# The decay exponentials of quarter 1 in front of the silu of z of quarter 1, in ScalarE's order of a delta-rule attention and FFN kernel

## What is computed

```python
mixed = silu(conv4(x @ W_qkv.T));  z = x @ W_z.T
q, k = l2norm(q), l2norm(k)
decay = exp(where(tril, gc[i] - gc[j], 0)) * tril          # gc: running sum of the log decay, in a chunk
A  = -(k_beta @ k.T * decay) * strict;  Tm = inv(I - A)
u  = Tm @ v_beta;  kcd = Tm @ (k_beta * exp(gc))
for each chunk:
    attn  = (q_i @ k_i.T) * decay_i
    v_new = u_i - kcd_i @ S
    out_i = (q_i * exp(g_i)) @ S + attn @ v_new
    S     = S * exp(g_last) + (k_i * exp(g_last - g_i)).T @ v_new
out = rmsnorm(out) * norm_w * silu(z);  y = out @ W_out.T
x = x + layernorm(y);  x = x + layernorm(ffn(layernorm(x)))
```

## Time and profile before

| | |
|---|---|
| time, median of 3 runs | 4530.6 us (4528.2 to 4533.37) |
| the profiled execution | 4533.44 us, of it 4531.0 us span |
| TensorE | 4297.6 us busy (95% of the span) |
| TensorE weight loads | 3229.5 us (71%) |
| VectorE | 3523.2 us (78%) |
| ScalarE | 2981.9 us (66%) |
| GpSimd | 2987.7 us (66%) |
| DMA | 275.17 MB, mean 61 GB/s |
| granted TensorE clock, mean | 0.985 |

### The profile page before, as it was taken

How to read it: one execution, slowest core, us unless ns; L and a number is a source line. 1 busy time by engine, 2 the same in 40 slices (tenths; PEclk the granted TensorE clock), 3 DMA queues, 4 the chain that set the end, 5 groups by cost and what they waited for, 6 DMA issues and landing times. The chain is left out here.

```text
span 4531.0 us, 93023 instructions
## 1 busy us (share of the span) xinstructions
PE 4297.6 (95%) x30676; PEld 3229.5 (71%) x30676; DVE 3523.2 (78%) x8064; ACT 2981.9 (66%) x6124; POOL 2987.7 (66%) x8711
## 2 busy tenths in 40 slices
PE   5899999999999999999999999999999999998898
PEld 2577777777777777777777777777777777776444
DVE  6688888888888888878888788878888888885554
ACT  3577777777777767766777767766777767774111
POOL 1677777777777777777777777777777777774000
PEclk7899999999999999999999999999999999999899
DMA  4222222222222222222222222222232222210200
GB/s 133 56 65 60 67 67 46 67 59 68 67 57 65 60 67 59 55 71 64 67 67 55 64 63 59 62 68 60 67 75 47 69 58 69 64 36 20 71 14 19
DMA packets 592240, 275.17 MB, mean 61 GB/s; under 512 B 464400, under 2 KB 548880, under 8 KB 582544
## 3 DMA queue, kind: packets, MB, share of 16 engines
q1 hardware_dynamic: 591040, 266.62, 23.9%
q0 software_dynamic: 720, 2.62, 0.3%
HBM read 221.84 MB, written 47.28 MB: 59 GB/s over the span
## 5 line engine op out<-in xcount | busy, mean ns | idle before, releaser
L714 DVE SCALAR_TENSOR_TENSOR CV<-pp,CW,CV 128x1023 f32<-128x1023 f32 (+2 forms) x768 | 980.3, 1276 | 33.1 <-ACT CV L1076 21.8
L339 PE MATMUL pp<-A,W 128*128 128x512 f32 x2048 | 970.4, 602 | 30.1 <-DVE CV L714 18.8
L1373 POOL TENSOR_TENSOR UL<-UL,TM 128x126 f32<-128x126 f32 (+22 forms) x1984 | 743.4, 375 | 155.4
L1370 POOL TENSOR_TENSOR TM<-UL,XL 128x126 f32<-128x126 f32 (+22 forms) x1984 | 708.5, 357 | 147.2 <-issue 12.6
L339 PEld LDWEIGHTS pp<-A,W 128*128 128x128 f32 x2048 | 377.7, 193 | 338.8 <-issue 307.2
L1172 ACT ACTIVATE QE<-qa,TAB 128x128 f32<-128x128 f32 x1024 | 318.2, 362 | 407.9 <-PE qa L468 407.8
L834 DVE SCALAR_TENSOR_TENSOR St<-St,TAB,kv 128x128 f32<-128x128 f32 x1024 | 309.0, 343 | 325.0 <-PE kv L487 317.2
L1183 ACT ACTIVATE VS<-qa,EB 128x128 f32<-128x128 f32 x1024 | 319.1, 364 | 300.5 <-PE qa L478 294.7
L510 PE MATMUL emit<-Wz,A 128*128 128x256 f32 x2048 | 492.0, 383 | 4.3 <-DVE A L885 4.1
L531 PE MATMUL emit<-Wo,NTr 128*128 128x256 f32 x2048 | 493.7, 384 | 1.3 <-ACT NTr L1216 1.3
L1076 ACT ACTIVATE CV<-pp,CW 128x1024 f32<-128x1024 f32 x256 | 285.0, 1113 | 231.2 <-PE pp L339 231.2
(11 more groups left out here) (220 smaller groups left out, 9242.3 us busy)
## 6 DMA issues: line engine op xcount, KB each, us to landing
GB<-gcd SPq DMA_DIRECT2D x64, 1024.0 KB, 4.9
W<-wqkv SPq DMA_DIRECT2D x256, 128.0 KB, 3.7
XL<-xb SPq DMA_DIRECT2D x128, 256.0 KB, 3.9
UL<-c_u SPq DMA_DIRECT2D x64, 256.0 KB, 2.9
xb<-X SPq DMA_DIRECT2D x512, 32.0 KB, 1.7
Wz<-wz SPq DMA_DIRECT2D x64, 256.0 KB, 2.8
ub<-UL SPq DMA_DIRECT2D x128, 128.0 KB, 2.9
N<-ub SPq DMA_DIRECT2D x256, 64.0 KB, 2.3
```

Source lines behind the costliest of these rows:

```text
L339: ins = t.matmul(bk.pp[:, 512 * h:512 * h + 512], m.W[:, c, k, :], m.xnT[:, w // KH % 2, c, 512 * h:512 * h + 512], start=c == 0, stop=c == 1)
L714: v.scalar_tensor_tensor(m.CV[:, t, d:S], bk.pp[:, 0:S - d], m.CW[:, w % KH, t, 3 - d:4 - d], m.CV[:, t, d:S], ALU.mult, ALU.add).then_inc ...
L1370: gp.tensor_tensor(m.TM[:, 0:a, 0:b], m.UL[:, 0:a, k:k + 1].to_broadcast([128, a, b]), m.XL[:, k, k + 1:32].unsqueeze(1).to_broadcast([128 ...
L1373: gp.tensor_tensor(m.UL[:, 0:a, k + 1:32], m.UL[:, 0:a, k + 1:32], m.TM[:, 0:a, 0:b], ALU.subtract).then_inc(s["sub"], 1)
```

## The change

In the body of ScalarE's loop the call `dec(u + 1, 1)` moves one place forward, ahead of `sz(u - 1, 1)`. (ScalarE's loop counts one iteration later than TensorE's, so these are the decay factors of one unit and the silu of the unit two before it.)

```diff
@@ -1306,8 +1306,8 @@
             dec(u + 1, 0)
             vs(u - 1, 5)
             vne(u - 1, 5)
+            dec(u + 1, 1)
             sz(u - 1, 1)
-            dec(u + 1, 1)
             qe(u - 1, 6)
             sq(u - 1, 2)
             nt(u - 1, 1)
```

## The result

| | before | after |
|---|---|---|
| median | 4531.8 us (4528.2 to 4533.4, 4 runs) | 4566.8 us (4565.1 to 4568.5, 4 runs) |
| ratio | | 1.008, 95% interval 1.0068 to 1.0092 |
| span of the profiled execution | 4531.0 us | 4562.7 us |

What follows compares the result with a forecast made beforehand. TensorE, busy 2929.0 of 3000 us, was taken as the bound. Terms +0.93, -0.22, -0.10 and +0.07 made +0.68 us a unit, times 62 about 43 us: 4574 us against the median 4530.6, range 4555 to 4602.

Steps and rivals of the forecast that it cites:

- silu of quarter 1 later: ScalarE, quarter 1: with the four exponentials first, the silu starts at 2098.43 instead of 2097.23, 1.20 us later.
- shift of TensorE behind the transpose: TensorE at L520: the transpose of `CO` waits for the later norm, +0.93 us a unit.
- given back at `op`: TensorE at `op`: it no longer waits for ScalarE's `NTr`, -0.22 us a unit.
- given back at `z` of quarter 2: TensorE at `z` of quarter 2: its wait for VectorE's `oacc` goes away, -0.10 us a unit.
- taken at the second transpose: TensorE, transpose of quarter 2: late exponentials of quarter 2 delay its norm, +0.07 us a unit.
- an undisturbed unit: One repeat of the loop, 63.22 us before: +0.68 us in all.
- 62 units: Loop counts 1 to 62, where the changed pair of calls exists in both forms: 62 x 0.68 = 42 to 43 us.
- The first wait: TensorE's weight load at L520, first transpose: waits for the norm, going from 2099.12 to 2100.22.
- all of the stall stays: Rival, 15%: nothing returned at `op` and `z`, or quarter 2 costs more; 1.1 us a unit, 68 us, 4599.
- a switch of tables saved for good: Rival, 1%: exponentials of quarter 2 1.3 us earlier than worked out, second transpose free; 0.61 us a unit, 38 us, 4568.
- The second path: Exponentials of quarter 2 over `x`, `att`, `core` and norm to the second transpose: 2.2 us late, costing +0.07 us a unit.
- side forecasts: The wrong one: moving quarter 3's exponentials ahead of quarter 2's silu in the kernel before makes no difference, 4526 to 4534.

Runs made afterwards that it cites:

- late silu alone: The changed kernel with the silu of quarter 1 replaced by a copy and a 1550-column scratch copy ahead of it; 4556.7 us, ratio 1.007 to before.
- three groups in a row: The changed kernel with the exponentials of quarter 2 also moved up, so quarters 0, 1 and 2 precede the silu of quarter 1; 4632.3 us, ratio 1.0232.
- the kernel with quarter 3 early: The kernel before with the exponentials of quarter 3 moved up behind those of quarter 2, ahead of its silu; 4511.7 us, ratio 0.9973.

## Why the prediction was right

The steps of the prediction beside the same steps in the trace of after (each counted from `z` of quarter 1, L510, and rounded, so that they add up to 0.61):

| step | predicted | measured |
|---|---|---|
| silu of quarter 1 later | 1.20 | 1.17 |
| shift of TensorE behind the transpose | +0.93 | +0.90 |
| given back at `op` | -0.22 | -0.22 |
| given back at `z` of quarter 2 | -0.10 | -0.11 |
| taken at the second transpose | +0.07 | +0.04 |
| an undisturbed unit | +0.68 | +0.60 |
| 62 units | +43 us | +37 us |
| whole kernel | +43 us | +35 us |

- **The mechanism** was the one forecast, and the experiment with the transpose moved in both kernels shows it: the change costs 35 us with the transpose where it was and 4 us with a projection ahead of it. The first wait is 1.09 us at the weight load, forecast 1.10.
- **The size** was 0.08 us a unit too large, in three small pieces: 0.03 at the silu (the exponentials' group takes 1.27 us, not 1.29), 0.03 at the second transpose, 0.01 at `z`, and the rest is rounding. The second transpose starts 16.21 us after `z` of quarter 1 (L510 at 2111.58 in the trace of after, 2127.79), where the earlier trace rows has 15.61: +0.60.
- **What was left out** is the units that are longer than the rest. The sum of what they have beyond the shortest unit is 19.6 us before and 14.7 us after. It brings the 37 us to the 32 by which the profiled spans differ. Most of the difference lies in two units (67.84 and 68.10 us long before, 67.77 and 65.00 after), and there in TensorE's wait for `W` (3.4 and 3.7 us before, 2.8 and 1.6 after). With the load of `W` moved, no unit in these two places is longer than 63.1 us. So these 5 us are for the most part waits for weights, at which the prediction did not look. Whether the change has a hand in them, or they differ from one execution to the next, is open.
- **The rival "all of the stall stays"** fell: `op` and `z` gave back 0.33 us, as their rows of before said.
- **The rival "a switch of tables saved for good"** has two runs near it. The late silu alone has its condition, no table load ahead of quarter 2, and was still 32 us slower (the rival says 38). In the three groups in a row two switches a unit were saved, and it was the slowest kernel of all. The Trainium skill's page "ScalarE: Activation LUTs", section "Table sets: the hidden batching unit", advises the grouping, and for ScalarE's own time it holds here (2981.9 us busy before, 2819.7 with two loads fewer a unit in the kernel with quarter 3 early). For the time of the kernel it decides nothing: with two loads fewer a unit the three groups are 103 us slower than before and the kernel with quarter 3 early is 13 us faster, since ScalarE's busy time is not what TensorE waits for.
- **The second path** was counted as +0.07 and stands in the table as +0.04, but that step is what is left of two things. In the kernel before, the second transpose already waits a little for its norm (the line below), and when TensorE comes late by the first path alone, it gets that back. The run with the late silu shows it: behind `z` of quarter 2 TensorE is 0.53 us later than in the kernel before, and the unit only 0.48 (middle of the undisturbed units in both traces). So -0.05 belongs at this transpose for the first path, and the second path adds 0.09 to it. The prediction names no return there, and that its last term came out near is in part luck.

```profile
2109.65 0.42 PEld L520 LDWEIGHTS emit<-cf,CO 128*128 128x128 f32 x4 [0.23 <-DVE CO L871]
```

- **One reading of the rows** is wrong in the prediction: of the 3000 us VectorE is busy 81%, not 74% or less (2441.01). Nothing in the sum hangs on it.
- **One of the side forecasts was wrong.** The expectation that the exponentials of quarter 3 would gain nothing looked at TensorE's waits for other engines only. The 26 waits for `W` stood in the same list, and the expectation did not ask what SyncE waits for.

## To carry to other kernels

Grouping activations by table is free only where the instruction that is pushed back has idle time ahead of it: look for the brackets in ScalarE's timeline (ahead of the silu no idle time in quarter 1, 1.41 us in quarter 2), and at how much later the step at the end of the chain may come without loss (the weight load of the transpose in quarter 1: about 0.1 us, since a silu 1.16 us later put it 1.06 us later). When an engine near its limit waits, follow every path that the edit makes later to the place where they meet again: the later one counts, not the sum. And before calling two paths independent, look whether one is late because of the other: here a third of the second path's delay came from the first. A compute step that gets earlier may pay through a transfer queue behind it, so read who waits for transfers before saying that nothing is gained.

## What the runs showed of the hardware

- After a wait, TensorE's first weight load and matmul start together and the group takes longer: eight matmuls of 256 columns 1.99 us instead of 1.89, four of 128 columns 0.66 instead of 0.60. A wait therefore costs up to 0.1 us more than its length.
- A table load took 1.28 us wherever the rows here show one, and an activation that waited for nothing started 0.01 or 0.02 us behind it, whether exponential or silu. The 2.66 us for a switch that the Trainium skill's page "ScalarE: Activation LUTs", section "What ACT_TABLE_LOAD costs", gives did not show. By an estimate from that figure, the exponentials of quarter 2 would have been some 3.5 us later. They were 2.1 us later (from `VN` of chunk 6 to their end 2.98 us after, 1.55 before, and `VN` itself 0.7 later with TensorE).
